# First attention stage in visits of two units: scores by head on half the rows of the array, no stacking by DMA

## The chip, the core and the metric

One core of one Trainium2 chip runs the whole program. The metric is the device time of the program in microseconds (us); for the kernel before, the median of three runs is 4077.31 us (4075.49 to 4078.02).

## What is computed

Sixteen samples of 512 tokens by 256 features pass through four blocks, each on a layer norm of its input and added to it. The change touches the first block alone:

```
x = x + attn_a(layernorm(x))      # 16 heads of width 64, gelu on the heads, then Wpost; X + P inside
x = x + ffn(layernorm(x))         # ternary weights, 256 -> 1024 -> 256
x = x + attn_b(layernorm(x))      # 16 heads of width 16, rotary, biases
x = x + ffn(layernorm(x))
...
Q, K, V = X @ Wq, X @ Wk, X @ Wv            # n, 512, 16, 64 each
attn = softmax(einsum('bshe,bthe->bsth', Q, K / 8), axis=2)
A = gelu(einsum('bsth,bthe->bshe', attn, V))
return X + A @ Wpost
```

## The kernel before

**Two stages.** The first stage does attn_a for all 16 samples and writes X1; the second does ffn, attn_b and ffn. Every engine runs one long loop over the same numbered slots, and each piece of work has a slot: `FIRST_A` to `LAST_A` for the first stage, from about slot 502 on also the opening of the second, whose scores begin at slot `SHIFT` = 554. Inside a slot the order is that of the code. Nothing reorders it, and engines wait for each other on semaphores.

**Units.** A sample has 8 pairs of heads; a pair has 4 units, a sample 32, the stage 512. Before, unit u of a pair is one head and one half of the queries (two blocks of 128). TensorE's slot s is: `a_scores(s + 3)` (4 matmuls of 512 columns), `a_transposes(s)` (8 of 128 columns, two banks), every fourth slot `a_values` of a whole pair (16 matmuls of 256 columns, which are 32 rows of the trace), then the products in `todo_of[s]`: queries or keys of a pair ("qk", 6 matmuls of 512), values of 128 tokens ("v", 6 of 512), transposed input ("x"), or the output product ("post", 24 of 256 columns for two blocks of tokens). Scores go to `ps_s`, four banks of PSUM, two to a unit, so that two units are in flight; everything else shares the three `banks`, filled in turn (`fill_of`), each waiting until the fill three before it is emptied.

**Exactness.** Products use fp32r parts: a high part and the rest. For the scores, ScalarE writes the high parts of q and k (L799) and VectorE the low parts (L972) to `raw_a`, with head 0 on partitions 0 to 63 and head 1 on 64 to 127. Six DMAs a pair (L364 to L366, `a_stack`) then build `stack_a`, where one head fills all 128 rows: high q above low q, against high k twice and low k twice. Two matmuls (L593, L594) give all four part products.

**The other engines, in slot s.** VectorE: `a_invert(s + 2)` (reciprocal of the sums, L954), the low parts or copies of the products of slot s - 1, `a_unit_max(s + 3)` (L947, 1024 columns), the copy of the first half of the transposed exponentials (L961, first of two banks), every fourth slot the copy of the values. ScalarE: the high parts or copies of slot s - 1, the copy of the second bank of transposed exponentials (L786), then `a_exps(s + 3)` (L775, two activations with running sums). GpSimd: the exponentials of unit s + 2 times the reciprocals (L495), which the transposes of slot s + 2 wait for. In this text the end of an instruction in a profile row is its start plus its duration.

## Time and profile before

| | |
|---|---|
| median of 3 runs | 4077.31 us |
| the profiled execution, its own time | 4078.41 us |
| its span, first to last instruction | 4076.6 us |
| mean granted TensorE clock | 0.981 of full |
| TensorE busy (matmuls overlap in this count) | 3760.2 us, 92% |
| first stage: last maximum taken (L947) | 2333.6 us |
| second stage: first maximum (L1088) | 2438.1 us |

The page slices the span in 40: TensorE is at 90% or more nearly everywhere but in the first slice and where the stages meet. Busy time counts a matmul from its start to the modelled end of its result, so neighbours overlap; how far one matmul is behind the last is read from the distance of their ends.

### The profile page before, as it was taken

Reading aid. Unit: us, or ns where it says so; the run is one execution under the profiler, and the core shown is the slowest. Engines: PE = TensorE matmul, PEld = TensorE weight load, DVE = VectorE, ACT = ScalarE, POOL = GpSimd, SP = SyncE. Lnnn points to the kernel's source line nnn. Section 1 sums busy time; section 2 is a strip of 40 time slices with the busy share of each in tenths; the row PEclk is TensorE's granted clock in tenths of the full one; section 3 lists DMA queues with packets and bytes.
Section 4 is the critical chain, followed back from the end, with each engine's and each line's share of the span. In section 5 each row is a group of like instructions: output and inputs, shape, how many; then the busy total and the mean of one; then the engine's idle time right before and its main releaser. Section 6 shows DMA issues by size and latency. Waiting matters only on the chain.

```text
span 4076.6 us, 64388 instructions
## 1 busy us (share of the span) xinstructions
PE 3760.2 (92%) x23170; PEld 2647.2 (65%) x23170; DVE 2718.1 (67%) x4275; ACT 2350.2 (58%) x4529; POOL 1930.6 (47%) x1219
## 2 busy tenths in 40 slices
PE   7999999999999999999999878999999999999987
PEld 5777777777777777777777654555555555555534
DVE  5665666666566666656666657777777777777762
ACT  4655655556555565555656535666666666666654
POOL 3454545445455455544544543444444444444412
PEclk9999999999999999999999978999999999999988
DMA  4443444434344344343443523232333332222220
GB/s 129 94 101 91 92 93 101 92 91 104 92 90 104 91 91 102 91 99 87 101 101 81 128 39 54 51 54 54 54 57 55 54 58 53 53 53 53 48 43 16
DMA packets 152363, 315.51 MB, mean 77 GB/s; under 512 B 23088, under 2 KB 76720, under 8 KB 152048
## 3 DMA queue, kind: packets, MB, share of 16 engines
q1 hardware_dynamic: 152048, 311.39, 35.6%
q8 instruction: 187, 3.06, 0.3%
q14 instruction: 128, 1.05, 0.1%
HBM read 33.43 MB, written 25.17 MB: 14 GB/s over the span
## 4 chain that ended last, share of the span: by engine, by line
PE 54%; DVE 21%; ACT 14%; issue 7%; POOL 3%; SPq 1%; DMA 0%; DVEq 0%; POOLq 0%; ACTq 0%
PE ps_o L622 10%; DVE neg_max L947 7%; ACT e_a L775 6%; PE ps_t L216 5%; PE ps_o L699 5%; DVE max_b L1088 4%; ACT raw_a L799 3%; PE ps_t L725 3%; PE ps_s L672 3%; PE ps_t L658 3%; PE ps_m L734 3%; PE ps_t L223 3%; PE ps_t L606 3%; PE ps_t L734 3%; POOL h_lo L529 2%
## 5 line engine op out<-in xcount | busy, mean ns | idle before, releaser
L495 POOL TENSOR_TENSOR e_a<-e_a,recip 128x1024 f32<-128x1024 f32 x512 | 970.4, 1895 | 1049.8 <-DVE recip L954 1049.8
L775 ACT ACTIVATE e_a<-ps_s,neg_max 128x512 f32<-128x512 f32 x1024 | 694.9, 684 | 245.0 <-DVE neg_max L947 234.1
L1088 DVE TENSOR_REDUCE max_b<-ps_s 128x2 f32<-128x1024 f32 x512 | 623.2, 1218 | 227.5 <-PE ps_s L672 225.1
L815 ACT ACTIVATE et<-ps_s 128x1024 f32<-128x1024 f32 x512 | 523.8, 1023 | 393.9 <-PE ps_s L686 393.8
L947 DVE TENSOR_REDUCE neg_max<-ps_s 128x2 f32<-128x1024 f32 x512 | 621.3, 1213 | 19.1 <-PE ps_s L594 19.1
L622 PE MATMUL ps_o<-et_a,v_a 128*64 128x256 f32 x4096 | 470.3, 382 | 0.0
L606 PE MATMUL ps_t<-ident,e_a 128*128 128x128 f32 x2736 | 394.7, 275 | 42.3 <-DVE et_a L961 36.1
L593 PE MATMUL ps_s<-stack_a 128*128 128x512 f32 x1024 | 412.7, 403 | 9.3 <-ACT e_a L775 7.7
L529 POOL TENSOR_TENSOR h_lo<-h,h_hi 128x512 fp32r<-128x512 f32 x256 | 327.2, 1296 | 168.8 <-ACT h_hi L859 168.8
L594 PE MATMUL ps_s<-stack_a 128*128 128x512 f32 x1024 | 401.9, 392 | 0.0
L606 PEld LDWEIGHTS ps_t<-ident,e_a 128*128 128x128 f32 x2736 | 321.2, 141 | 111.2 <-DVE et_a L961 52.1
L622 PEld LDWEIGHTS ps_o<-et_a,v_a 128*64 128x64 f32 x4096 | 282.5, 137 | 151.1 <-issue 21.4
L786 ACT ACTIVATE et_a<-ps_t 128x512 f32<-128x512 f32 x339 | 202.5, 597 | 297.1 <-PE ps_t L606 297.1
L954 DVE RECIPROCAL recip<-sums 128x2 f32<-128x2 f32 x512 | 84.7, 165 | 400.9 <-ACT e_a L775 400.9
L672 PE MATMUL ps_s<-k_stack,q_stack 48*128 48x512 f32 x1024 | 262.2, 508 | 91.8 <-DVE max_b L1088 91.5
L517 POOL TENSOR_TENSOR rstd<-rstd,minus_half 128x4 f32<-128x4 f32 x48 | 49.4, 1029 | 512.3 <-DVE rstd L1059 512.1
L699 PE MATMUL ps_o<-et,v_b 128*32 128x512 f32 x2048 | 283.6, 627 | 0.0
L972 DVE SCALAR_TENSOR_TENSOR raw_a<-ps_t,raw_a 128x512 fp32r<-128x512 f32 x171 | 118.3, 692 | 243.5 <-ACT raw_a L799 242.1
L672 PEld LDWEIGHTS ps_s<-k_stack,q_stack 48*128 48x128 f32 x1024 | 99.4, 188 | 257.6 <-issue 139.7
L961 DVE COPY et_a<-ps_t 128x512 f32<-128x512 f32 x345 | 235.0, 681 | 0.0
L593 PEld LDWEIGHTS ps_s<-stack_a 128*128 128x128 f32 x1024 | 192.8, 188 | 54.0 <-ACT e_a L775 13.1
L606 PE MATMUL ps_m<-ident,e_a 128*128 128x128 f32 x1360 | 207.3, 275 | 19.3 <-DVE et_a L961 16.9
(198 smaller groups left out, 7939.6 us busy)
## 6 DMA issues: line engine op xcount, KB each, us to landing
stack_a<-raw_a SPq DMA_DIRECT2D x256, 384.0 KB, 4.7
stack_a<-raw_a SPq DMA_DIRECT2D x256, 256.0 KB, 4.3
stack_a<-raw_a SPq DMA_DIRECT2D x256, 128.0 KB, 3.5
q_stack<-roped_q SPq DMA_DIRECT2D x256, 64.0 KB
k_stack<-roped_k SPq DMA_DIRECT2D x256, 64.0 KB
x_a<-X SPq DMA_DIRECT2D x16, 512.0 KB, 3.7
X<-x_a SPq DMA_DIRECT2D x16, 512.0 KB, 2.9
x_ahead<-X SPq DMA_DIRECT2D x16, 512.0 KB, 3.8
```

The lines of the kernel that those rows point to most:

```text
L495: nc.gpsimd.tensor_tensor(e_a[:, u % 4, :, :], e_a[:, u % 4, :, :], factor, ALU.mult).then_inc(e_normed, 1)
L529: nc.gpsimd.tensor_tensor(h_lo[:, i, :], h32[:, n % 4, :], h_hi[:, i, :], ALU.subtract).then_inc(h_split, 1)
L593: mm(out, st[:, 0, c:c + P], st[:, 1, :], start=True, stop=False)
L594: last = mm(out, st[:, 0, c:c + P], st[:, 2, :], start=False, stop=True)
L606: last = nc.tensor.transpose(bank(fill)[:, c:c + P], e_a[:, u % 4, j, t * P:(t + 1) * P], ident[:, :])
L622: last = mm(ps_o[HA * h:HA * (h + 1), half * HS:(half + 1) * HS], v_a[:, t, c:c + HA], et_a[:, (4 * n + 2 * half + h) % 5, t, :], start=(t ...
L672: last = mm(ps_s[:, score_bank(u) + h, :], q_stack[rows, pair, block_ * P:(block_ + 1) * P], k_stack[rows, pair, :], start=True, stop=True)
L699: last = mm(ps_o[32 * h:32 * (h + 1), :], v_b[:, s % 2, keys, 4 * quad + h, :], et[:, (2 * w + h // 2) % 5, h % 2, :], start=(keys == 0), ...
L775: ins = nc.scalar.activation(e_a[:, u % 4, j, :], ps_s[:, 2 * (u % 2) + j, :], ACT.Exp, bias=neg_max[:, u % 4, j:j + 1], accum_out=sums[:, ...
L815: nc.scalar.activation(et[:, v % 5, :, :], ps_s[:, 2:4, :], ACT.Exp)\
L947: nc.vector.reduce_max(neg_max[:, u % 4, :], ps_s[:, 2 * (u % 2):2 * (u % 2) + 2, :], AX.X, negate=True)\
L1088: nc.vector.reduce_max(max_b[:, u // 4 % 2, :, u % 4], ps_s[:, score_bank(u):score_bank(u) + 2, :], AX.X, negate=True).then_inc(max_done, 1)
```

## The change

**Visits.** A unit is now one block of 128 queries of both heads. `a_scores(u)` runs in even slots for units u and u + 1: per unit 6 matmuls with 64 rows each, head 0 on rows 0 to 63 and head 1 on rows 64 to 127, straight from `raw_a`, for three of the four part products (low times low is left out). `a_stack`, `stack_a` and their DMAs are gone. A visit writes all four banks of `ps_s`, so it waits until the exponentials of the unit before it are done (`a_exp_done >= u`), where before it waited for those of two units back. Values run in odd slots for two units (8 matmuls of 256 columns, 16 rows of a trace). `LEAD` = 4 takes the place of 3, and reciprocals and GpSimd's product stay at s + 2.

**Products.** Queries are made in slots 1 mod 4, keys in slots 2 mod 4, and values and output products in slots 0 and 3 mod 4, so that nearly every slot has one product of 6 or 12 matmuls; "post" is one block of tokens a fill. In slots 4 and 20 of a sample VectorE copies both banks.

**Setting up.** ScalarE casts four of the six pieces of the first weights. Input buffers are three. The weights of the ffn are loaded at slot 40, their sums taken at 471 and 473, their thresholds at 475 (509 before) and their quantising at 504 and 506 (509 and 510 before).

```diff
-        XT, QK_FIRST, VALUE_SLOTS = -10, -8, ((-6, -5, -2, -1), (3, 3, 7, 15))
-        POST = ((27, 31), (42, 43))
+        XT, QK_SLOTS = -9, (-7, -6)
+        FIRST_VALUES, VALUE_SLOTS = (-5, -4, -1, 0), ((-8, -5, -4, -1), (7, 8, 15, 16))
+        POST, LAST_POSTS = ((32, 32, 35, 36), (43, 44, 51, 52)), (45, 46, 47, 48)
...
+        GELUS, BOTH_TURNED = (19, 35), (4, 20)
...
-        LOAD_W1, LOAD_W2, LOAD_WB, SPLIT, ABS = 500, 503, 506, (511, 512), (503, 506)
-        GAMMA, QUANTISE, SCALE, CLEAR = 508, (509, 510), 514, (513, 514)
-        FIRST_SPLIT, SPLIT_OF_PAIR = (-12, -9, -6, -5, -4, -3), ((1, 2), (4, 5))
+        LOAD_W, LOAD_WB, LOAD_REST, SPLIT, ABS = 40, 484, 503, (508, 509), (471, 473)
+        GAMMA, QUANTISE, SCALE, CLEAR = 474, (504, 506), 514, (513, 514)
+        FIRST_CAST, FIRST_SPLIT, SPLIT_OF_PAIR = (None, None, -8, -5, -4, 5), (-11, -8, -7, -4, -2, 6), ((1, 2), (4, 5))
...
                 def a_scores(u):
-                    n, half, h = u // 4, u // 2 % 2, u % 2
+
+                    n = u // 4
                     if u % 4 == 0:
-                        pe.wait_ge(stacked[n % 2], (n // 2 + 1) * 6 * 16)
-                    if u >= 2:
-                        pe.wait_ge(a_exp_done, u - 1)
-                    st = stack_a[:, n % 2, h, :, :]
+                        for i in range(2):
+                            wait_emptied(pe, fill_of["qk", n % PAIRS, i, n // PAIRS])
+                    if u:
+                        pe.wait_ge(a_exp_done, u)
+                    raw = raw_a[:, n % 2, :, :]
                     for j in range(2):
-                        c = (2 * half + j) * P
-                        out = ps_s[:, 2 * (u % 2) + j, :]
-                        mm(out, st[:, 0, c:c + P], st[:, 1, :], start=True, stop=False)
-                        last = mm(out, st[:, 0, c:c + P], st[:, 2, :], start=False, stop=True)
-                    last.then_inc(a_qk_done, 1)
+                        c = (u % 4 + j) * P
+                        for m, (q_part, k_part) in enumerate(((0, 2), (0, 3), (1, 2))):
+                            for h in range(2):
+                                rows = slice(HA * h, HA * (h + 1))
+                                last = mm(ps_s[:, 2 * j + h, :], raw[rows, q_part, c:c + P], raw[rows, k_part, :],
+                                          start=(m == 0), stop=(m == 2))
+                        last.then_inc(a_qk_done, 1)
...
-                        if 0 <= slot + 3 < UNITS_ALL:
-                            a_scores(slot + 3)
+                        if slot % 2 == 0 and 0 <= slot + LEAD < UNITS_ALL:
+                            a_scores(slot + LEAD)
+                        if slot % 2 == 1 and 3 <= slot < UNITS_ALL:
+                            a_values((slot - 3) // 2)
+                        if slot == UNITS_ALL:
+                            a_values(UNITS_ALL // 2 - 1)
                         if 0 <= slot < UNITS_ALL:
                             a_transposes(slot)
-                        if slot % 4 == 0 and 1 <= slot // 4 <= PAIRS * BATCH:
-                            a_values(slot // 4 - 1)
...
-                        if 0 <= slot < UNITS_ALL:
+                        if 0 <= slot < UNITS_ALL and slot % UNITS not in BOTH_TURNED:
                             a_copy_turned(slot)
-                        if 0 <= slot + 3 < UNITS_ALL:
-                            a_exps(slot + 3)
+                        if 0 <= slot + LEAD < UNITS_ALL:
+                            a_exps(slot + LEAD)
...
-                        if 0 <= slot + 2 < UNITS_ALL:
-                            a_invert(slot + 2)
+                        if slot % 2 == 1 and 0 <= slot + LEAD < UNITS_ALL:
+                            a_unit_max(slot + LEAD)
+                        if 0 <= slot + LEAD - 2 < UNITS_ALL:
+                            a_invert(slot + LEAD - 2)
                         for todo in todo_of.get(slot - 1, []):
                             a_low(todo)
-                        if 0 <= slot + 3 < UNITS_ALL:
-                            a_unit_max(slot + 3)
+                        if slot % 2 == 0 and 0 <= slot + LEAD < UNITS_ALL:
+                            a_unit_max(slot + LEAD)
```

TensorE in the middle of the stage, before: a slot with scores of one unit, transposes and the values of a whole pair, and the product after them (`stack_a` holds the stacked parts, `et_a` the transposed exponentials).

```order
L593 MATMUL ps_s<-stack_a 128x512
L594 MATMUL ps_s<-stack_a 128x512
L593 MATMUL ps_s<-stack_a 128x512
L594 MATMUL ps_s<-stack_a 128x512
L606 MATMUL ps_t<-ident,e_a 128x128 x8
L622 MATMUL ps_o<-et_a,v_a 64x256 x16
L216 MATMUL ps_m<-xh_a,wa_hi 128x512
L216 MATMUL ps_m<-xh_a,wa_lo 128x512
L216 MATMUL ps_m<-xh_a,wa_hi 128x512
L216 MATMUL ps_m<-xh_a,wa_lo 128x512
L216 MATMUL ps_m<-xl_a,wa_hi 128x512 x2
L593 MATMUL ps_s<-stack_a 128x512
```

TensorE there in the changed kernel: an even slot (scores of two units, transposes, keys), then an odd slot up to its product.

```order
L592 MATMUL ps_s<-raw_a 128x512 x12
L605 MATMUL ps_t<-ident,e_a 128x128 x8
L216 MATMUL ps_m<-xh_a,wa_hi 128x512
L216 MATMUL ps_m<-xh_a,wa_lo 128x512
L216 MATMUL ps_m<-xh_a,wa_hi 128x512
L216 MATMUL ps_m<-xh_a,wa_lo 128x512
L216 MATMUL ps_m<-xl_a,wa_hi 128x512 x2
L623 MATMUL ps_o<-et_a,v_a 64x256 x8
L605 MATMUL ps_t<-ident,e_a 128x128 x8
L223 MATMUL ps_m<-wa_hi,xh_a 128x512
```

Scores of two units now stand together every second slot, with values of two units in the slots between, and one product stands between the odd slot's transposes and the next scores.

ScalarE at the same place, before:

```order
L775 ACTIVATE e_a,sums<-ps_s,neg_max 128x512 x2
L799 ACTIVATE raw_a<-ps_t 128x512
L786 ACTIVATE et_a<-ps_m 128x512
L775 ACTIVATE e_a,sums<-ps_s,neg_max 128x512 x2
L786 ACTIVATE et_a<-ps_m 128x512
```

ScalarE in the changed kernel:

```order
L777 ACTIVATE e_a,sums<-ps_s,neg_max 128x512 x2
L803 ACTIVATE raw_a<-ps_m 128x512
L784 ACTIVATE et_a<-ps_t 128x512
L777 ACTIVATE e_a,sums<-ps_s,neg_max 128x512 x2
L803 ACTIVATE raw_a<-ps_m 128x512
```

The kinds stand in the same order: the copy of the transposed exponentials (L786, now L784) goes ahead of the exponentials of its slot in both. What moved is what waits for them: the exponentials of an odd slot now release the next scores.

VectorE, before, three slots:

```order
L954 RECIPROCAL recip<-sums 128x2
L972 SCALAR_TENSOR_TENSOR raw_a<-ps_t,raw_a 128x512
L947 TENSOR_REDUCE neg_max<-ps_s 128x2
L961 COPY et_a<-ps_t 128x512
L954 RECIPROCAL recip<-sums 128x2
L947 TENSOR_REDUCE neg_max<-ps_s 128x2
L961 COPY et_a<-ps_t 128x512
```

VectorE in the changed kernel, an even slot from its low part on, and the odd slot after it:

```order
L981 SCALAR_TENSOR_TENSOR raw_a<-ps_t,raw_a 128x512
L956 TENSOR_REDUCE neg_max<-ps_s 128x2
L970 COPY et_a<-ps_t 128x512
L999 COPY heads_a<-ps_o 128x512
L956 TENSOR_REDUCE neg_max<-ps_s 128x2
L963 RECIPROCAL recip<-sums 128x2
L981 SCALAR_TENSOR_TENSOR raw_a<-ps_t,raw_a 128x512
L970 COPY et_a<-ps_t 128x512
```

In odd slots the maximum (L956) has moved ahead of the reciprocal and of the low part.

## Rows read from the trace of the kernel before

**Rows 1.** The page: busy us (share of the span) and instructions; one costly group.

```profile
PE 3760.2 (92%) x23170; PEld 2647.2 (65%) x23170; DVE 2718.1 (67%) x4275; ACT 2350.2 (58%) x4529; POOL 1930.6 (47%) x1219
...
L947 DVE TENSOR_REDUCE neg_max<-ps_s 128x2 f32<-128x1024 f32 x512 | 621.3, 1213 | 19.1 <-PE ps_s L594 19.1
```

**Rows 2.** Busy time by stretch, second sample: PE, PEld, DVE, ACT, POOL, clock, DMA.

```profile
182.20:327.20 145.00, 137.48 (x889) 107.50 (x888) 90.92 (x153) 84.39 (x193) 74.33 (x42) 1.00 0.42 95
```

**Rows 3.** TensorE's waits, 100 to 2230 us: us in total, times, longest.

```profile
PE ps_t L606 <- DVE et_a L961: 31.7, 60, 0.7
...
PE ps_s L593 <- DMA stack_a<-raw_a: 0.2, 1, 0.2
```

**Rows 4.** Timeline of TensorE: the same matmul eleven samples apart (start, duration).

```profile
557.02 0.50 PE L593 MATMUL ps_s<-stack_a 128*128 128x512 f32 x1 [0.23 <-ACT e_a L775]
...
2151.87 0.50 PE L593 MATMUL ps_s<-stack_a 128*128 128x512 f32 x1 [0.23 <-ACT e_a L775]
```

**Rows 5.** Timeline of TensorE: product, scores of a unit, transposes.

```profile
1003.78 0.62 PE L216 MATMUL ps_t<-xl_a,wa_hi 128*128 128x512 f32 x2
...
1004.93 0.40 PE L594 MATMUL ps_s<-stack_a 128*128 128x512 f32 x1
...
1005.60 0.60 PE L606 MATMUL ps_m<-ident,e_a 128*128 128x128 f32 x4
```

**Rows 6.** Timeline of TensorE: into the values of a pair and out.

```profile
1012.72 0.66 PE L606 MATMUL ps_m<-ident,e_a 128*128 128x128 f32 x4 [0.31 <-DVE et_a L961]
1013.31 3.67 PE L622 MATMUL ps_o<-et_a,v_a 128*64 128x256 f32 x32
1016.92 0.50 PE L216 MATMUL ps_t<-xh_a,wa_hi 128*128 128x512 f32 x1
```

**Rows 7.** Timeline of TensorE, second stage: matmuls of 48 and 50 rows in twos.

```profile
3002.50 0.27 PE L742 MATMUL ps_t<-ident,max_b 128*8 128x128 f32 x1
3002.70 0.50 PE L672 MATMUL ps_s<-k_stack,q_stack 48*128 48x512 f32 x2
3003.04 0.40 PE L686 MATMUL ps_s<-q_stack,k_stack 50*128 50x512 f32 x2
```

**Rows 8.** Timeline of TensorE, second stage: values in column quarters, then transposes.

```profile
2595.78 1.06 PE L699 MATMUL ps_o<-et,v_b 128*32 128x512 f32 x8
2596.77 0.66 PE L719 MATMUL ps_t<-ident,xn 128*128 128x128 f32 x4
```

**Rows 9.** Timeline of TensorE: transposes, and the last of 24 output matmuls.

```profile
1026.65 0.60 PE L606 MATMUL ps_m<-ident,e_a 128*128 128x128 f32 x4
...
1029.84 0.28 PE L658 MATMUL ps_t<-wpost_hi,heads_parts 128*128 128x256 f32 x1
```

**Rows 10.** Timeline of ScalarE just after: the copy, then a unit's exponentials.

```profile
1027.29 0.60 ACT L786 ACTIVATE et_a<-ps_m 128x512 f32<-128x512 f32 x1 [0.43 <-PE ps_m L606]
1027.78 0.68 ACT L775 ACTIVATE e_a<-ps_s,neg_max 128x512 f32<-128x512 f32 x1
...
1029.02 0.21 ACT L775 ACTIVATION_READ_ACCUMULATOR e_a<-ps_s,neg_max 128x1 f32 x1
```

**Rows 11.** Timeline: the end of a unit's exponentials, ahead of 557.02 above.

```profile
556.77 0.20 ACT L775 ACTIVATION_READ_ACCUMULATOR e_a<-ps_s,neg_max 128x1 f32 x1
```

**Rows 12.** Timeline at the start: VectorE's low part, then TensorE.

```profile
18.69 0.69 DVE L972 SCALAR_TENSOR_TENSOR raw_a<-ps_t,raw_a 128x512 fp32r<-128x512 f32 x1 [1.64 <-ACT raw_a L799]
```

**Rows 13.** Timeline of TensorE at the start: first value product, first transposes.

```profile
22.99 0.77 PE L223 MATMUL ps_t<-wa_hi,xh_a 128*128 128x512 f32 x1 [4.96 <-DVE wa_lo L927]
```

**Rows 14.** The same, slot 0.

```profile
41.17 0.73 PE L606 MATMUL ps_t<-ident,e_a 128*128 128x128 f32 x4
```

**Rows 15.** Timeline of TensorE: transposes of slots 480 and 504.

```profile
2212.08 0.60 PE L606 MATMUL ps_m<-ident,e_a 128*128 128x128 f32 x4
...
2315.08 0.60 PE L606 MATMUL ps_m<-ident,e_a 128*128 128x128 f32 x4
```

**Rows 16.** Timeline of TensorE where the stages meet: slot 511, first "up" product.

```profile
2345.98 1.11 PE L606 MATMUL ps_t<-ident,e_a 128*128 128x128 f32 x4 [5.38 <-DVE xl L1131]
...
2358.05 0.74 PE L725 MATMUL ps_m<-xh,w 128*128 128x512 f32 x2
```

**Rows 17.** Timeline of VectorE there: one quantising pass.

```profile
2342.37 2.35 DVE L1028 SCALAR_TENSOR_TENSOR w<-w_raw,half_gamma,w 128x2048 fp32r<-128x2048 f32 x1
```

223 lines of the change are left out of this document (111 added, 112 removed).

## The prediction, made before the changed kernel ran

> **What bounds the kernel now.** I read the busy times first: TensorE has 92% [rows 1], and in one sample of the first stage 137.5 of 145.0 us [rows 2]. That count overlaps, so the next view is the timeline, where I take distances between the ends of matmuls. The same matmul stands at 557.02 and at 2151.87 us, eleven samples apart [rows 4]: 1594.85 / 11 = 144.99 us a sample. The stage repeats to a few hundredths, so it can be summed.
>
> Pitches: 512 columns take 0.23 us (1004.40 to 1004.63, and scores of a unit end at 5.33: 4 in 0.93) [rows 5]. Eight transposes take 6.20 - 5.33 = 0.87, 0.109 each. Twenty-four output matmuls take 1030.12 - 1027.25 = 2.87, 0.12 each [rows 9]. The values of a pair take 1016.98 - 1013.38 = 3.60 [rows 6]. Their 32 rows are 16 steps; with a step of 0.216 the first costs 0.36, so 0.14 goes for entering the mode with two column halves, and the product behind ends its first matmul 0.44 later where 0.23 is usual: 0.21 for leaving it.
>
> A sample's work on TensorE before, then: 32 x (0.93 + 0.87) + 8 x 3.81 = 88.1 for scores, transposes and values; 24 products of 6 x 0.23 = 1.38 (16 queries and keys, 8 values) = 33.1; output 96 x 0.12 = 11.5; x 8 x 0.11 = 0.9. Sum 133.6. The other 11.4 us are waits, and the table of waits shows the main one: transposes that wait until VectorE has emptied a bank [rows 3], in slots with little work on TensorE. The stacking DMAs cost almost nothing (0.2 us) [rows 3].
>
> **The change part by part.**
>
> *Scores.* Two units took 1.86 us. Now there are six steps of two matmuls on half the rows each. That such twos run side by side the second stage shows: two matmuls end at 3003.20 and the next two at 3003.44, a step of 0.24 [rows 7]. Entering costs: the first two end 0.43 after a 128-column matmul, 0.19 more than a step. Leaving a tiled mode for transposes: the four end at 2597.43, 0.59 after the values; less 3 x 0.109 the first took 0.26, so 0.15 more [rows 8]. Sum: 0.43 + 5 x 0.24 + 0.15 = 1.78. Gain 0.08 for two units, of the quarter of the matmuls that the change drops.
>
> *Values.* 0.36 + 7 x 0.216 + 0.15 = 2.02 for two units, where half of 3.81 is 1.90: loss 0.12, since the mode is entered twice as often. Together TensorE's work is 0.04 us a pair of slots larger, 16 x 0.04 = 0.6 a sample: 134.2. Products are only moved. So any gain has to come from the 11.4 us of waits.
>
> The Trainium skill, TensorEngine Tiling (Array Packing), Key Properties, gives row tiling up to twice the speed, but says that changing the mode drains TensorE. The trace agrees that both hold (0.24 for two, 0.15 to 0.21 at a change).
>
> *Old waits.* They go: with scores and values in turn and one product of 1.38 to 1.44 us in nearly every slot, no slot is as short as the bare 1.80 us of scores and transposes, and VectorE's copy (after a 1.21 us maximum [rows 1]) comes before the bank is needed.
>
> *The new wait.* Scores of slot s + 2 need all four banks of `ps_s`, so the exponentials of the odd slot s + 1 must be done. ScalarE does them behind the copy of that slot's second bank, which needs the last transpose of slot s + 1. On TensorE only the odd product (1.38) stands between. This ring is closed by waits alone, whatever slack the engines have:
> - last transpose to start of copy: 1027.25 to 1027.29, 0.04 [rows 9, 10];
> - copy to exponentials behind it: 0.49 [rows 10];
> - exponentials to the end of their sum: 1027.78 to 1029.23, 1.45 [rows 10];
> - that end (556.97) to the end of the first score matmul (557.52): 0.55 [rows 4, 11].
>
> In all 2.53. Without the wait it would be 1.38 + 0.43 = 1.81, so 0.72 us stand idle in each pair of slots, 16 x 0.72 = 11.5 a sample, as much as the old waits were. The whole ring: 2.53 + 5 x 0.24 (less 0.01 of rounding in the step, 1.19) + transposes 0.26 + 7 x 0.109 = 1.02, + the even product, + values 1.87 + transposes 1.02 = 7.63 + even product. Even products of a sample: 8 keys and 4 values of 1.38, 5 output blocks of 1.44: 23.7. A sample: 16 x 7.63 + 23.7 = 145.8, against 145.0. From slot 32 to slot 480 are 14 samples: **+11 us**.
>
> *The opening.* Slot 0 transposes at 41.17 [rows 14]. Value weights were split by VectorE alone, and TensorE waited 4.96 us until 22.99 [rows 13]. ScalarE's casts take that wait away, and the scores no longer wait for DMAs: the low part of the first keys is there at 19.38 [rows 12], the first scores go behind one value product at about 20.6. Two rounds of score, maximum, second maximum behind a split, exponentials (1.0 + 1.2 + 1.2 + 2 x 1.45 + 0.5, about 7 each) and one visit of 1.6 lead to 36: **-5 us** (bounds -2 and -8). Slots 0 to 32 then lack five output blocks on the ring and have one value product more: 16 x 7.63 + 17.9 = 140.0, where 182.2 - 41.2 = 141.0 were [rows 2, 14]: **-1**.
>
> *The end.* From slot 480 [rows 15] the ring takes 12 x 7.63 + 18.2 = 109.8 to slot 504, where 2315.08 - 2212.08 = 103.0 were: +7. From 504 to the first "up" 43.0 passed [rows 15, 16], with TensorE waiting 5.38 at once behind thresholds and quantising (2.35 for one of its passes [rows 17]). Now these lie under slots 475 to 506, where a quantising of 3.6 delays the second maximum by some 1.6 in each of two visits: 2 x 9.2 + some 12 for slots 508 to 511 = 30, **-13**. Together **-6** (bounds +1 and -12). Behind that nothing changes: the second stage keeps its order, and the same 48 output matmuls come there.
>
> Third input buffer, earlier loads of X and of weights, smaller output adds, two more bank copies on VectorE: nothing, since VectorE is busy 91 of 145 us and ScalarE 84 [rows 2]. If that cover fails it shows in the ring, below.
>
> **Sum.** +11 - 5 - 1 - 6 = -1 on 4078.4, the profiled execution's own time; the median of the runs is 1.1 below that. I predict **4076 us**: no change that a measurement of this kernel can tell, which needs about 0.2% or 8 us.
>
> **The rivals.**
>
> *Faster by a shorter ring.* The ring turns 256 times, so 0.05 us in it is 13 us. Its softest term is the step of two matmuls: 0.24 [rows 7], but tiled values step at 0.216 for the same streaming time [rows 6]. With that: 5 x 0.024 x 256 = 31 less, 4045. For it: tiled mode. Against: the one row of the same kind. The ends of the two openings, both guessed short of work, add up to 9 more. Chance 0.24.
>
> *The change does what its layout suggests.* If the exponentials do not gate the next visit, a sample falls to 134.2: 15 x 10.8 + 7 = 170 less, 3906. It needs the odd product to cover 2.1 us (2.53 - 0.43); it is 1.44 at most. Chance 0.03.
>
> *Slower: the heads of visits.* A visit of values now waits for four bank copies and, every second time, for the copy of the last values; the changes of mode are eight in four slots where there were two. If leaving and entering a mode on the ring (three times in a pair of slots) costs the 0.21 seen behind the values [rows 6] and not 0.14 to 0.15, this adds 3 x 0.06 x 256 = 46: 4122; half of it, 4099. It decides from 0.03 us a turn on. Against: rows 8 show the very change into transposes. The Trainium skill, TensorE: Matmul & The Clock Gate, Single matmul latency, gives a fixed cost of 166 ns at full clock for a matmul that nothing overlaps; taken as the price of a change, an estimate from that page is 3 x 0.02 x 256 = 15 us more. Chance 0.23.
>
> *Slower: VectorE late for the values.* The values wait until the last ones are copied out of `ps_o`. I find that copy done some 0.4 us before TensorE comes, once in four slots. With VectorE 1 us later it costs 0.6 x 128 = 77: 4153. Chance 0.08.
>
> **How the numbers follow.** The forecast has 0.42, within 8 us. Faster has 0.24 + 0.03 and slower 0.23 + 0.08, about 0.27 and 0.31. The range leaves out the 170 and the 77 and some of each end: 4045 to 4110.
>
> **What the profile after would show.** A sample of 145.8 us from one score matmul to the same 32 units on; every even slot's first score matmul waiting about 0.6 us for ScalarE's exponentials; nearly no wait of transposes for VectorE's copy; twos of score matmuls 0.24 apart; slot 0 at 36 and first "up" near 2357. I am wrong if the ring is not closed as I wrote it (scores released by something else), or if a sample is off by over 0.6 us.

## The result, and the profile after

| | before | after |
|---|---|---|
| median, timed side by side | 4076.40 us (4 runs, 4075.45 to 4078.02) | 4102.61 us (4 runs, 4100.78 to 4107.73) |
| span of the profiled execution | 4076.6 us | 4099.0 us |
| granted TensorE clock | 0.981 | 0.981 |

The ratio is 1.0066, with a 95% interval of 1.0048 to 1.0083: the kernel is slower by 26 us, where 4076 and no measurable change were forecast. The time lies inside the range of 4045 to 4110. The two profiled executions are 22.4 us apart; the other 4 us between the medians lie in runs without a profile.

The page after: busy times, the chain that ended last, and the group that answers to L947 of [rows 1].

```profile
PE 3725.7 (91%) x24194; PEld 2520.5 (61%) x24194; DVE 2733.9 (67%) x4367; ACT 2299.7 (56%) x4501; POOL 1921.2 (47%) x1219
...
PE 68%; ACT 12%; DVE 12%; issue 5%; POOL 3%; DMA 0%; ACTq 0%; DVEq 0%; POOLq 0%
...
L956 DVE TENSOR_REDUCE neg_max<-ps_s 128x2 f32<-128x1024 f32 x512 | 623.3, 1217 | 159.7 <-PE ps_s L592 159.7
```

VectorE sat idle 19.1 us ahead of its maxima before [rows 1] and sits idle 159.7 now, for scores. ScalarE has 12% of the chain that ended last. The second sample by stretch, as in [rows 2], and TensorE's waits from 100 to 2230 us (total, times, longest), as in [rows 3]:

```profile
174.70:321.10 146.40, 135.31 (x955) 99.55 (x953) 91.88 (x159) 80.77 (x191) 73.88 (x43) 1.00 0.03 8
```

```profile
PE ps_s L592 <- ACT e_a L777: 157.0, 225, 2.1
PE ps_s L592 <- DVE v_a L988: 5.0, 7, 0.7
```

A sample takes 146.4 us (145.0 before), the DMA share fell from 0.42 to 0.03, and the transposes no longer wait for VectorE. One wait is left: the score matmuls (L592) for ScalarE's exponentials (L777), at the head of nearly every visit. It is the ring that the prediction describes: a chain of waits that comes back to its own start once in every two slots. Here it is closed twice, in TensorE's timeline and ScalarE's (start, duration), from an odd slot's transposes to the next scores:

```profile
1205.69 0.60 PE L605 MATMUL ps_m<-ident,e_a 128*128 128x128 f32 x4
...
1208.32 1.66 PE L592 MATMUL ps_s<-raw_a 64*128 64x512 f32 x12 [0.63 <-ACT e_a L777]
1209.91 0.65 PE L605 MATMUL ps_t<-ident,e_a 128*128 128x128 f32 x4
...
1214.69 0.60 PE L605 MATMUL ps_m<-ident,e_a 128*128 128x128 f32 x4
...
1217.41 0.74 PE L592 MATMUL ps_s<-raw_a 64*128 64x512 f32 x4 [0.69 <-ACT e_a L777]
```

```profile
1206.33 0.60 ACT L784 ACTIVATE et_a<-ps_m 128x512 f32<-128x512 f32 x1 [3.83 <-PE ps_m L605]
1206.83 0.68 ACT L777 ACTIVATE e_a<-ps_s,neg_max 128x512 f32<-128x512 f32 x1
...
1208.06 0.21 ACT L777 ACTIVATION_READ_ACCUMULATOR e_a<-ps_s,neg_max 128x1 f32 x1
...
1217.06 0.21 ACT L777 ACTIVATION_READ_ACCUMULATOR e_a<-ps_s,neg_max 128x1 f32 x1
```

The transposes end at 1206.29, the copy starts at 1206.33, the exponentials at 1206.83, their sum ends at 1208.27, the scores start at 1208.32. The next visit differs in one thing: sum at 1217.27, scores at 1217.41, 0.14 behind it and not 0.05. Over the stage's 255 visits behind the first the two kinds take turns, but for one visit: 126 with 0.143 to 0.145, 128 with 0.052 or 0.053. The first kind is the one in which `a_scores` also waits for the emptied query and key banks.

**Where the 22.4 us between the spans are**, from the first transposes of slots 0, 32, 480 and 504, the first "up" and the first maximum of the second stage:

| stretch | before | after | difference | forecast |
|---|---|---|---|---|
| start to slot 0 | 41.2 | 33.9 | -7.3 | -5 |
| slot 0 to 32 | 141.1 | 140.8 | -0.3 | -1 |
| 32 to 480, 14 samples | 2029.8 | 2049.6 | +19.8 | +11 |
| 480 to 504 | 103.0 | 110.7 | +7.7 | +7 |
| 504 to the first "up" | 43.0 | 43.3 | +0.3 | -13 |
| to the second stage's first maximum | 80.1 | 82.1 | +2.0 | 0 |
| rest | 1638.5 | 1638.6 | +0.1 | 0 |

Two forecasts failed: the samples by 9 us, and the end by 15. The opening is less certain than its line looks. From slot 0 to slot 32 the kernels of experiments 5 to 8 run the same code as this one; two of them took 140.7 us at a granted clock of 1.00, as here, and two 143.3 and 143.4 at 0.98.

The end, VectorE and GpSimd after, where [rows 16] and [rows 17] stood before:

```profile
2350.42 2.35 DVE L1037 SCALAR_TENSOR_TENSOR w<-w_raw,half_gamma,w 128x2048 fp32r<-128x2048 f32 x1
...
2357.01 2.35 DVE L1011 CAST wb_hi<-wb_raw 128x768 fp32r<-128x768 f32 x2
...
2359.94 5.29 DVE L1016 TENSOR_TENSOR wb_lo<-wb_raw,wb_hi 128x768 fp32r<-128x768 f32 x2
```

```profile
2359.51 1.89 POOL L486 TENSOR_TENSOR e_a<-e_a,recip 128x1024 f32<-128x1024 f32 x1 [1.04 <-DVE recip L963]
2361.36 3.05 POOL L516 TENSOR_TENSOR x_ahead<-x_ahead,b_rows 128x1024 f32<-128x1024 f32 x1
```

Quantising no longer stands at the very end, but the split does (5.29 us for two subtractions), and TensorE's transposes of slot 510 wait 5.9 us behind it:

```profile
PE ps_s L592 <- ACT e_a L777: 7.0, 4, 3.6
PE ps_t L605 <- DVE xl L1140: 5.9, 1, 5.9
PE ps_t L605 <- DVE et_a L970: 2.5, 1, 2.5
```

These are TensorE's waits from 2310 to 2385 us. Its clock differs there too. Busy time by stretch, before and after, with the granted clock as the third number from the end:

```profile
2315.00:2358.00 43.00, 32.38 (x236) 24.88 (x233) 34.90 (x51) 14.12 (x34) 18.10 (x12) 0.92 0.35 96
2335.00:2378.00 43.00, 29.25 (x187) 20.84 (x187) 29.39 (x39) 11.33 (x26) 15.44 (x9) 0.82 0.03 6
```

With levels of 1.2 and 2.4 GHz, 0.82 means that TensorE ran some 15 us of these 43 at the lower one, and 0.92 some 7; after, each of these stretches begins in or just behind a wait of 2.1 to 5.9 us. Two groups of matmuls on the chain that ended last show the price: scores of 2.61 us, and values of 3.48 us behind the wait of 5.9, where 1.66 and 1.95 are usual.

```profile
2343.57 2.61 PE L592 MATMUL ps_s<-raw_a 64*128 64x512 f32 x12 [3.60 <-ACT e_a L777]
...
2368.13 3.48 PE L623 MATMUL ps_o<-et_a,v_a 128*64 128x256 f32 x16
```

### The profile page after: what moved, and what is told of

It is laid out like the page before. It is cut to its first block, busy times and chain, and to the rows that moved or that the text cites. A ratio compares the mean times of both kernels' runs of the same rounds, so it can differ in the third digit from the quotient of the medians.

```text
span 4099.0 us, 65128 instructions
## 1 busy us (share of the span) xinstructions
PE 3725.7 (91%) x24194; PEld 2520.5 (61%) x24194; DVE 2733.9 (67%) x4367; ACT 2299.7 (56%) x4501; POOL 1921.2 (47%) x1219
## 4 chain that ended last, share of the span: by engine, by line
PE 68%; ACT 12%; DVE 12%; issue 5%; POOL 3%; DMA 0%; ACTq 0%; DVEq 0%; POOLq 0%
PE ps_o L623 12%; PE ps_s L592 10%; ACT e_a L777 9%; PE ps_t L605 8%; PE ps_o L699 4%; DVE max_b L1097 4%; PE ps_m L605 4%; PE ps_t L216 4%; PE ps_t L734 4%; PE ps_s L672 3%; PE ps_t L725 2%; PE ps_t L658 2%; PE ps_m L216 2%; PE ps_s L686 2%; PE ps_m L725 2%
## 5 line engine op out<-in xcount | busy, mean ns | idle before, releaser
L956 DVE TENSOR_REDUCE neg_max<-ps_s 128x2 f32<-128x1024 f32 x512 | 623.3, 1217 | 159.7 <-PE ps_s L592 159.7
L777 ACT ACTIVATE e_a<-ps_s,neg_max 128x512 f32<-128x512 f32 x1024 | 692.1, 686 | 9.9 <-DVE neg_max L956 9.5
L592 PE MATMUL ps_s<-raw_a 64*128 64x512 f32 x3072 | 427.1, 408 | 184.5 <-ACT e_a L777 179.3
L784 ACT ACTIVATE et_a<-ps_t 128x512 f32<-128x512 f32 x299 | 179.0, 599 | 652.4 <-PE ps_t L605 652.4
L623 PE MATMUL ps_o<-et_a,v_a 128*64 128x256 f32 x4096 | 501.1, 387 | 2.4 <-DVE heads_a L999 1.7
L592 PEld LDWEIGHTS ps_s<-raw_a 64*128 64x128 f32 x3072 | 291.6, 185 | 305.9 <-ACT e_a L777 140.6
L623 PEld LDWEIGHTS ps_o<-et_a,v_a 128*64 128x64 f32 x4096 | 274.1, 137 | 191.0 <-issue 73.1
L970 DVE COPY et_a<-ps_t 128x512 f32<-128x512 f32 x366 | 252.1, 691 | 203.6 <-PE ps_t L605 199.3
L605 PEld LDWEIGHTS ps_t<-ident,e_a 128*128 128x128 f32 x2660 | 291.3, 141 | 139.0 <-issue 121.9
L784 ACT ACTIVATE et_a<-ps_m 128x512 f32<-128x512 f32 x181 | 108.4, 599 | 398.9 <-PE ps_m L605 398.9
L734 PE MATMUL ps_t<-w,h_hi 128*128 128x256 f32 x752 | 203.1, 305 | 25.9 <-POOL h_lo L522 25.7
L605 PE MATMUL ps_m<-ident,e_a 128*128 128x128 f32 x1436 | 224.8, 279 | 0.0
```

Of the source, the lines that this page charges most:

```text
L592: last = mm(ps_s[:, 2 * j + h, :], raw[rows, q_part, c:c + P], raw[rows, k_part, :], start=(m == 0), stop=(m == 2))
L605: last = nc.tensor.transpose(bank(fill)[:, c:c + P], e_a[:, u % 5, j, t * P:(t + 1) * P], ident[:, :])
L623: last = mm(out, v_a[:, t, c:c + HA], et_a[:, 2 * (q % 2):2 * (q % 2) + 2, t, h, :], start=(t == 0), stop=(t == TB - 1))
L734: last = mm(half, hidden[:, f, tokens], w2[:, f, :], start=(f == 0 and m == 0), stop=(f == FT - 1 and m == 1))
L777: ins = nc.scalar.activation(e_a[:, u % 5, h, :], ps_s[:, 2 * (u % 2) + h, :], ACT.Exp, bias=neg_max[:, u % 5, h:h + 1], accum_out=sums[:, ...
L956: nc.vector.reduce_max(neg_max[:, u % 5, :], ps_s[:, 2 * (u % 2):2 * (u % 2) + 2, :], AX.X, negate=True)\
```

## The experiments

All but one start from the kernel after. Each was timed beside the kernel before, whose medians were 4078.6 to 4080.2 us here and 4076.4 in the result above. Times of different series can so be compared to about 4 us, and the ratio to the kernel before stands beside each. The sample that is given is the mean from slot 32 on, without the stage's last.

**1. Exponentials first.** Two lines of ScalarE's loop change places, in odd slots.

```diff
+                        if slot % 2 == 1 and 0 <= slot + LEAD < UNITS_ALL:
+                            a_exps(slot + LEAD)
                         if 0 <= slot < UNITS_ALL and slot % UNITS not in BOTH_TURNED:
                             a_copy_turned(slot)
-                        if 0 <= slot + LEAD < UNITS_ALL:
+                        if slot % 2 == 0 and 0 <= slot + LEAD < UNITS_ALL:
                             a_exps(slot + LEAD)
```

> The kernel after, but in odd slots ScalarE does the exponentials ahead of its copy of turned exponentials (in even slots the copy stays first). Theory (the sample's length is set by a ring: last transpose, ScalarE's copy, exponentials, end of their sum, first score matmul, then TensorE's work up to the next last transpose): the last transposes and the copy leave the ring, TensorE stops waiting 1.1 us each second slot, a sample falls from 146.4 to 134 to 137 us, and the time to 3930 to 3970 us. Rival A (the second maximum, not the copy, holds the exponentials): a sample stays at 145 to 147, the time at 4090 to 4105. Rival B (the copy is now late by the 1.1 to 1.4 us of the exponentials, and the values or the next transposes wait for it on TensorE, since the bank that it frees is wanted back): the wait only changes its name to ScalarE's copy, a sample of 141 to 150, the time 4030 to 4150.

Measured: 3929.1 us, ratio 0.9632 (0.9618 to 0.9647). The second sample and the largest of TensorE's waits from 100 to 2230 us:

```profile
161.30:296.50 135.20, 134.62 (x955) 98.66 (x953) 91.95 (x159) 81.99 (x191) 73.98 (x43) 1.00 0.03 9
```

```profile
PE ps_s L592 <- ACT e_a L777: 8.8, 3, 6.2
PE ps_m L658 <- POOL heads_parts L490: 5.2, 1, 5.2
```

The theory holds. A sample takes 135.1 us, and the wait of 157.0 us is gone but for the end. What was moved is only the order of two instructions on an engine that is 56% busy; the mean durations of the costly groups changed by 1% or less (an exponential takes 692 ns, 686 before). One small group did not: VectorE's cast for the output product takes 602 ns and not 508. ScalarE's rows show the new order: the exponentials of the odd slot start 2.0 us ahead of the copy, before that slot's last transposes are done.

```profile
1212.59 0.70 ACT L777 ACTIVATE e_a<-ps_s,neg_max 128x512 f32<-128x512 f32 x1
...
1213.25 0.71 ACT L777 ACTIVATE e_a<-ps_s,neg_max 128x512 f32<-128x512 f32 x1
...
1214.58 0.60 ACT L784 ACTIVATE et_a<-ps_t 128x512 f32<-128x512 f32 x1 [0.53 <-PE ps_t L605]
```

**2. The second wait of the visit's head, a slot earlier.**

```diff
 def a_scores(u):
-    if u % 4 == 0:
+    if u == 0:
         for i in range(2):
-            wait_emptied(pe, fill_of["qk", n % PAIRS, i, n // PAIRS])
+            wait_emptied(pe, fill_of["qk", 0, i, 0])
...
 a_transposes(slot)
+if slot % 4 == 3 and 0 < slot + 5 < UNITS_ALL:
+    n = (slot + 5) // 4
+    for i in range(2):
+        wait_emptied(pe, fill_of["qk", n % PAIRS, i, n // PAIRS])
```

> The kernel after, but the wait for the two emptied query and key banks, which stood at the head of every other visit together with the wait for the exponentials, is made on TensorE one slot earlier, behind the transposes of the odd slot before. Theory (the second wait at the head costs 0.064 us in each visit that has it, on the ring): 128 x 0.064 = 8 us less, 4094 us; first score matmul of those visits 0.054 behind the sum's end and not 0.144. Rival (the 0.064 comes from what TensorE did before, products of half width, and not from the second wait): no change, 4102, the first score matmul still 0.11 to 0.15 behind the sum's end. Second rival: the banks are emptied late, and the earlier wait holds the products of that slot: slower, 4110 or more.

Measured: 4096.8 us, ratio 1.0047 (1.0034 to 1.0059). In time that is 6 us less, near the edge of what five runs tell. The trace is sharper: 248 of 255 visits now start 0.053 us behind the sum, and a sample takes 145.58 us, 0.81 less (8 x 0.09 = 0.72 by the two distances). The 14 samples are 11.2 us shorter; slot 32 comes 5.9 us later, half of it between slots 0 and 32 at a granted clock of 0.98 and not 1.00, which hides part of the gain. So the wait at the head costs 0.09 us of its own, although the banks had long been empty. With it gone the ring is 0.2 us a sample from what was forecast (145.8).

**3. and 4. A shorter product beside the ring, and one in it.** For the queries (b = 0, third experiment) or the keys (b = 1, fourth), two matmuls of six (the low parts are left out, so the products are less exact):

```diff
-last = feature_major(bank(fill), xh_a, xl_a, wa_hi, wa_lo, b * DA + a * P)
+if b == 0:
+    for k in range(KT):
+        last = mm(bank(fill), wa_hi[:, k, b * DA + a * P:b * DA + a * P + P], xh_a[:, k, :],
+                  start=(k == 0), stop=(k == KT - 1))
+else:
+    last = feature_major(bank(fill), xh_a, xl_a, wa_hi, wa_lo, b * DA + a * P)
```

> The kernel after, but of the queries' product, which stands in an odd slot behind the last transposes, 2 matmuls of 6 are done (those of the high parts alone; the low parts of queries' input and weights are left out). Theory (ring): that product lies beside the ring, behind the last transpose and ahead of the wait for the exponentials, and not in it; TensorE only waits 0.9 us more there: a sample of 146 to 147 as before, the time 4095 to 4103. Rival (TensorE's own work sets the sample): 4 x 0.23 = 0.92 us less in 8 visits a sample, 139 a sample, 4103 - 118 = 3985 us.

Measured: 4104.9 us, ratio 1.0065 (1.0047 to 1.0084), a sample of 146.4, and the wait for exponentials grew from 157.0 to 254.6 us. 118 us of TensorE's work taken away give nothing: that work lies beside the ring, and TensorE's busy time as such does not bound the stage.

> The kernel after, but of the keys' product, which stands in an even slot between the score matmuls and the transposes of the odd slot, 2 matmuls of 6 are done (those of the high parts alone; the low parts are left out). Theory (ring): that product is in the ring, so all of it counts: 4 x 0.23 = 0.92 us less in 8 visits a sample, 146.4 - 7.4 = 139.0 a sample, the time 4103 - 118 = 3985 us. Rival (VectorE's maxima or copies set the sample, and TensorE's work is hidden): less than half of it, 4045 us or more.

Measured: 4076.4 us, ratio 0.9997 (0.9987 to 1.0007), a sample of 144.58. Only 1.8 of the 7.4 us a sample came back, less than half, as the rival had it. TensorE's waits, and VectorE's and TensorE's rows at one odd slot:

```profile
PE ps_s L592 <- ACT e_a L782: 139.3, 204, 2.1
PE ps_o L623 <- DVE heads_a L1004: 49.9, 88, 0.6
PE ps_o L623 <- ACT et_a L789: 25.6, 30, 1.0
PE ps_s L592 <- DVE v_a L993: 21.7, 30, 0.7
```

```profile
1212.81 1.21 DVE L961 TENSOR_REDUCE neg_max<-ps_s 128x2 f32<-128x1024 f32 x1
1214.01 0.69 DVE L975 COPY et_a<-ps_t 128x512 f32<-128x512 f32 x1
1214.62 0.68 DVE L1004 COPY heads_a<-ps_o 128x512 f32<-128x512 f32 x1
```

```profile
1214.16 0.71 PE L647 MATMUL ps_t<-xh_a,wa_hi 128*128 128x512 f32 x2
1215.44 0.87 PE L623 MATMUL ps_o<-et_a,v_a 128*64 128x256 f32 x6 [0.57 <-DVE heads_a L1004]
```

The keys' product covered VectorE's copies between the scores and the values of the next slot. With 0.92 us of cover gone the values wait 0.57 for the copy out of `ps_o`: a second limit stands some 0.35 us behind the ring in these slots (0.92 - 0.57, an estimate). This is the prediction's last rival, VectorE late for the values, which found that copy some 0.4 us early.

**5. to 8. The end.** First, the last sample's output products put in among its last visits, and the split of the second stage's weights three slots earlier:

```diff
-where = LAST_POSTS if late(s, half) else POST[half]
+where = LAST_POSTS if late(s, half) else (27, 29, 30, 31) if (s, half) == (BATCH - 1, 0) else POST[half]
```

> The kernel after, but the output products of the last sample's first half stand in the slots 27, 29, 30 and 31 of that sample (507, 509, 510 and 511) and not in 512, 512, 515 and 516. Theory (24 of these 48 matmuls lay behind the last unit ahead of the first ups, 24 among the ups, and the last visits' waits hide them where they are put now): 48 x 0.12 = 5.7 us less, 4097 us, the first up 3 us nearer to the last unit. Rival (the end waits for VectorE's low part of the last inputs, not for TensorE's work, so that only the place of the wait changes): within 2 us of 4102.6.

Measured: 4110.9 us, ratio 1.0078 (1.0066 to 1.0091), on the wrong side of both. TensorE's waits at the end:

```profile
PE ps_s L592 <- ACT e_a L777: 4.9, 1, 4.9
PE ps_t L605 <- DVE x_a L993: 4.5, 1, 4.5
PE ps_m L605 <- DVE xl L1140: 2.0, 1, 2.0
PE ps_t L658 <- DVE xl L1140: 1.9, 1, 1.9
```

An output product fills a bank that VectorE must add out (L993), and that add stands behind the 5.29 us of the split. By the trace the second stage begins 3.2 us later for it. Another 7 us of this run lie in the second stage, whose code is the same; they are told of below.

```diff
-        LOAD_W, LOAD_WB, LOAD_REST, SPLIT, ABS = 40, 484, 503, (508, 509), (471, 473)
+        LOAD_W, LOAD_WB, LOAD_REST, SPLIT, ABS = 40, 484, 503, (505, 507), (471, 473)
```

> The kernel after, but VectorE splits the second stage's weights in slots 505 and 507, not in 508 and 509. Theory (in the kernel after, the cast took 2.35 us and the subtraction 5.29, beside GpSimd's instructions, against 1.02 and 1.82 in the kernel before; the transposes of slot 510 waited 5.9 us for VectorE behind it): with the two kinds farther apart the cast takes 1.0 to 1.3 and the subtraction 1.8 to 3, the wait at slot 510 falls below 2 us, and the time to 4096 to 4099. Rival A (VectorE is full from 504 on: quantising, 3.7 us a piece, fills it anyway): the maxima of slots 505 to 508 come later by what the splits take, and the time stays within 2 us of 4102.6 or goes up by as much as 5. Rival B (the long duration belongs to the instruction and its operands' places, not to GpSimd): still 2.35 and 5.29.

Measured: 4098.5 us, ratio 1.0049 (1.0036 to 1.0062). The rows of VectorE:

```profile
2344.69 1.88 DVE L1011 CAST wb_hi<-wb_raw 128x768 fp32r<-128x768 f32 x1
...
2358.75 1.81 DVE L1016 TENSOR_TENSOR wb_lo<-wb_raw,wb_hi 128x768 fp32r<-128x768 f32 x2
```

The subtractions take 0.94 us each where no GpSimd instruction runs beside them, and rival B falls. The cast met one even here (1.88 us for the first of two that take 1.02 together alone). The wait at slot 510 fell from 5.9 to 2.0 us, and from the transposes of slot 504 to the first "up" 39.0 us pass, not 43.3.

Then the quantising too, moved behind the last maximum:

```diff
-        LOAD_W, LOAD_WB, LOAD_REST, SPLIT, ABS = 40, 484, 503, (508, 509), (471, 473)
-        GAMMA, QUANTISE, SCALE, CLEAR = 474, (504, 506), 514, (513, 514)
+        LOAD_W, LOAD_WB, LOAD_REST, SPLIT, ABS = 40, 484, 503, (504, 506), (471, 473)
+        GAMMA, QUANTISE, SCALE, CLEAR = 474, (509, 510), 514, (513, 514)
```

> The kernel after with VectorE's jobs of the last slots in another order: the weights are split in slots 504 and 506 (2.3 us together where GpSimd is idle, up to 7.6 beside it), and the feed-forward weights quantised in 509 and 510, behind the last maximum (slot 507), and not in 504 and 506. Theory (quantising, 3.6 us a piece, delays the maxima of slots 504 to 507, so that TensorE waits 3.6 and 2.1 us for exponentials; behind the last maximum it only holds copies and the low part of the last inputs, as it did in the kernel before): those two waits fall to 1.2 and less, the first up 3 to 6 us earlier against the rest of the stage, 4095 to 4100. Rival (the work is the same, and what it no longer holds at 504 it holds at 509 and 510): within 2 us of 4102.6, waits of 3 us or more for VectorE's copies at slots 509 to 511.

Measured: 4099.9 us, ratio 1.0050 (1.0037 to 1.0064); the stretch takes 41.8 us. The waits for exponentials fell as the theory says (5.5 us in all, none above 2.1), but VectorE's jobs now meet GpSimd's (a second quantising pass takes 4.31 us beside it, 2.35 alone) and hold the last inputs' low part for longer. It is the rival that came out, in this row:

```profile
PE ps_t L605 <- DVE xl L1140: 6.8, 1, 6.8
```

Last, the work itself: the second pass of each quantising is left out, so the feed-forward weights are no longer the reference's.

```diff
-link(nc.vector.tensor_scalar(out, flat, half_gamma[:, 1, i:i + 1], None, ALU.is_lt))
-nc.vector.scalar_tensor_tensor(out, flat, half_gamma[:, 0, i:i + 1], out, ALU.is_gt, ALU.subtract)\
-    .then_inc(weights_ready, 1)
+nc.vector.tensor_scalar(out, flat, half_gamma[:, 1, i:i + 1], None, ALU.is_lt).then_inc(weights_ready, 1)
```

> The kernel after, where quantising does only its first pass of two for each weight matrix (the second, 2.35 us on VectorE each in slots 504 and 506, is left out, so the weights of the feed-forward layers aren't the reference's). Theory (VectorE sets the end of the first stage from slot 504 on): of 4.7 us at least 3 come back between the transposes of slot 504 and the first up (43.3 in the kernel after), 4096 to 4100, and TensorE's waits of 3.6 and 2.1 us for the exponentials there fall to 1.3 and less. Rival (TensorE's own work, half of it at a granted clock of 0.8, sets it and the waits are made up for elsewhere): 43.3 within 1 us, the time within 2 us of 4102.6.

Measured: 4094.2 us, ratio 1.0041 (1.0027 to 1.0055). The stretch takes 38.5 us: of 4.7 us taken from VectorE, 4.8 came back, at the same granted clock (0.82). So VectorE's work counts in full there. The waits for exponentials fell from 5.7 to 2.5 us, not to 1.3; the wait for the low part stayed at 5.9 us, since the split was not touched. The amount of work is not all of it: VectorE is busy 26.0 us in this stretch in experiment 6 and 26.1 in experiment 7, and they take 39.0 and 41.8 us. Its jobs' places count too.

**9. and 10. Two parts of the change undone**, each on the kernel after.

```diff
-a_normalise_exps(slot + LEAD - 2)
+a_normalise_exps(slot + LEAD - 1)
...
-a_invert(slot + LEAD - 2)
+a_invert(slot + LEAD - 1)
```

> The kernel after with one part of the change undone: the reciprocals (VectorE) and the multiplications by them (GpSimd) one slot earlier. Theory (the ring doesn't run through the reciprocals: they are done two slots ahead of the transposes, and VectorE finds the sums ready within 0.2 us of the end of its maximum): a sample of 146.0 to 146.8, the time 4098 to 4108. Rival (VectorE now stops for the exponentials with its copies and maxima queued behind it, which was the reason for the later slot): waits of VectorE for ScalarE of 0.5 us or more a slot, a sample of 148 or more, 4130 us or more.

Measured: 4106.0 us, ratio 1.0062 (1.0047 to 1.0077), a sample of 146.37. VectorE does stop for the exponentials, 389.2 us in all, and the sample shows that TensorE is not held by it.

```diff
-if slot % 2 == 1 and 0 <= slot + LEAD < UNITS_ALL:
-    a_unit_max(slot + LEAD)
...
-if slot % 2 == 0 and 0 <= slot + LEAD < UNITS_ALL:
+if 0 <= slot + LEAD < UNITS_ALL:
     a_unit_max(slot + LEAD)
```

> The kernel after with one part of the change undone: the second maximum of a visit isn't first in its slot on VectorE, but behind the reciprocal and the low parts, as the first one is. Theory (the exponentials of odd slots start at the end of ScalarE's copy, 2.8 us behind the end of their maximum, so 0.15 to 0.85 us on it are hidden): a sample of 146.2 to 146.8, the time 4100 to 4106. Rival (the maximum is the gate that the profile doesn't name): up to 128 x 0.7 = 90 us more, 4130 us or more.

Measured: 4108.7 us, ratio 1.0068 (1.0051 to 1.0084), a sample of 146.28. The time is above the 4100 to 4106 of the theory, but this isn't in the samples. The profiled execution is 11 us longer: 6 us up to slot 32, half of it from slot 0 on at a granted clock of 0.98, then 2 less up to the second stage, and 7 in that stage, whose code is the same. Neither part does anything to a sample while the ring is closed.

**11. The kernel before, exponentials first in every slot.**

```diff
+if 0 <= slot + 3 < UNITS_ALL:
+    a_exps(slot + 3)
 if 0 <= slot < UNITS_ALL:
     a_copy_turned(slot)
-if 0 <= slot + 3 < UNITS_ALL:
-    a_exps(slot + 3)
```

> The kernel before, with ScalarE's exponentials ahead of its copy of turned exponentials in every slot, as the one edit. Theory (in the kernel before no ring ran through the exponentials; TensorE waited for VectorE's copies and for its own order, 11.4 us a sample, and a later copy on ScalarE can only hold the values): no gain, a sample of 145 to 150, the time 4070 to 4150. Rival (the order copy first costs either kernel the same): the sample falls to 135 to 138, the time to 3930 to 3970 as in the kernel after.

Measured: 4228.0 us, ratio 1.0365 (1.0346 to 1.0384), a sample of 154.3. ScalarE's largest wait there, and the same wait in the kernel before:

```profile
ACT e_a L775 <- DVE neg_max L947: 743.8, 413, 4.5
```

```profile
ACT e_a L775 <- DVE neg_max L947: 201.9, 251, 1.4
```

The edit that takes 4% from the kernel after adds 4% to the kernel before. There every slot makes the scores, the maximum and the exponentials of one unit in turn, so exponentials in front wait for the maximum of their own slot, and the copy with its bank waits behind them. ScalarE's rows show the first; how it reaches TensorE is argued, since TensorE's listed waits from 100 to 2230 us grew by only some 60 us (113 to 173), of which 29 are for that copy. In the kernel after, an odd slot's scores are made a slot earlier. It is worse than the 4150 of the theory, whose direction was right. Which part of the change (two units a visit, `LEAD` of 4, the earlier second maximum) makes the order bearable was argued here, not told apart.

**12. Exponentials first in even slots too.**

```diff
+if 0 <= slot + LEAD < UNITS_ALL:
+    a_exps(slot + LEAD)
 if 0 <= slot < UNITS_ALL and slot % UNITS not in BOTH_TURNED:
     a_copy_turned(slot)
-if 0 <= slot + LEAD < UNITS_ALL:
-    a_exps(slot + LEAD)
```

> The kernel after, with ScalarE's exponentials ahead of its copy in every slot, even slots too. Theory (in an even slot the exponentials wait for the first maximum, 2.9 us behind the first score matmul, so the copy behind them ends about 4.9 us behind it, where the transposes of the odd slot want its bank at 4 to 6): slower than with odd slots alone, TensorE waits for ScalarE's copy, 3950 to 4060 us. Rival (it has slack enough): 3925 to 3935, as with odd slots alone. Other rival (the copy of even slots joins a ring of its own): above 4102.

Measured: 3925.5 us, ratio 0.9620 (0.9601 to 0.9639), a sample of 135.14, the same as with odd slots alone. The rival with slack enough came out. By the order of the code, the bank of the even slot's copy is not wanted back before the odd slot's transposes are through, with values and a product between.

**13. to 15. Together.** Experiments 1, 2 and 5:

> Three edits on the kernel after together: exponentials ahead of the copy in odd slots, the wait for the query and key banks made a slot earlier, and the last sample's first output products in slots 507 to 511. Theory (with the ring open TensorE hardly waits, 35 us in the whole first stage, so the second edit has nothing left to shorten, and the third takes 3 to 6 us at the end): 3923 to 3928, against 3929 for the first edit alone. Rival (the ring was only loosened, and its second wait still counts): 3915 to 3920. Other side: the early wait holds TensorE where it has no slack now, 3932 or more.

Measured: 3933.8 us, ratio 0.9643 (0.9628 to 0.9657). The other side came out, but for experiment 5's reason: the waits for the add of the output product (3.9 us) and for the low part (3.9) are in this trace too, and a sample is unchanged (135.17). Experiments 1 and 6:

> The two edits that gained alone, together on the kernel after: exponentials ahead of the copy in odd slots, and the second stage's weights split in slots 505 and 507. Theory (the one works in all sixteen samples, the other in the last eight slots, and they share no wait): 3929 - 4 = 3925, within 3921 to 3929, and the subtraction of the split at 0.94 us apiece. Rival (with the ring open TensorE reaches the end sooner than VectorE, which is then the one that is late there, so that the split's place counts otherwise): 3931 or more.

Measured: **3920.4 us**, ratio 0.9609 (0.9595 to 0.9624), 4% below the kernel before and the fastest here, 0.6 us under the range of the theory. From slot 504 to the first "up" 41.1 us pass, 45.7 in experiment 1, and the subtractions take 0.94 us each. Then the quantising last and the split in 504 and 506:

> The fastest so far (exponentials ahead of the copy in odd slots, split in slots 505 and 507; 3920) with quantising moved behind the last maximum (509 and 510) and the split to 504 and 506. Theory: the one wait of 6.2 us for the exponentials at slot 504 falls to 1 or 2, 3914 to 3918. Rival (the copies of slots 509 to 511 now wait for VectorE): 3918 to 3924.

Measured: 3925.3 us, ratio 0.9624 (0.9611 to 0.9637). Against the one before, the intervals overlap and the first "up" stands at 2197.7 and at 2197.0: no gain, as experiment 7 lets one expect. The time is outside both the theory's 3914 to 3918 and the rival's 3918 to 3924. The wait for exponentials fell from 6.2 only to 3.5 us, and the one for the low part rose from 2.0 to 7.2.

## Why the prediction was wrong, step by step

- *What bounds the kernel, pitches, TensorE's work.* Right. In the rows above, the scores end at 1209.98, four transposes 0.58 later, where 0.26 + 3 x 0.109 = 0.59 was worked out. TensorE's work was put at 134.2 us a sample; with the ring open a sample takes 135.1, which leaves costly changes of mode 0.9 us of the 2.9 that this rival gave them, at most.
- *Old waits, new wait.* Right: the first went, the second came, with the four pieces 0.04, 0.50, 1.44 and the start behind the sum.
- *The ring's length.* This term was mis-sized, since the end of the sum to the first score matmul was read at one visit of the kernel before and taken for all. In every second visit the head has a second wait, which costs 0.09 us. Experiment 2 takes it out and finds 145.58, where 145.8 was forecast. In the kernel after it is 146.39, just inside the 0.6 us that the prediction allowed itself: +19.8 us for 14 samples, not +11.
- *The rival with the shorter ring (0.24), and the one in which the exponentials don't gate (0.03).* The first did not come. The second is excluded for this kernel by the 157.0 us, but its price was near: a sample of 134.2 and a time of 3906 were worked out, and experiment 1 measured 135.1 and 3929. The prediction saw that the copy stands ahead of the exponentials and summed it as fixed. It didn't ask which of the two has slack, which the trace before couldn't show but the ring's own list could: the copy is wanted a slot later than the exponentials.
- *The opening.* -7.3 where -5 with bounds of -2 and -8 was given. Right. That slots 0 to 32 came out within 1 us is in part luck: the same code took 2.6 us more in two other executions, at a lower granted clock.
- *480 to 504.* +7.7 where +7 was given. Right.
- *504 to the first "up".* This is the step that failed: -13 was forecast and +0.3 came. It summed TensorE's visits (2 x 9.2 + 12) and let VectorE's jobs vanish beneath the maxima. The split of the weights, moved from 511 and 512 to 508 and 509, isn't in the sum at all; it took 7.6 us, where it took 2.8 before. Experiment 6, which takes most of that back, shortens the stretch by 4.3 us, and experiment 8 shows what VectorE's work costs there: 4.7 us less work, 4.8 us less time. VectorE is busy 29.4 of the 43 us, and what it does comes in chains with TensorE (scores, maximum, exponentials), so that the other jobs lengthen the chains. The sum also took TensorE at full clock. The lower clock costs 2.5 us in the two groups shown above, a part of the miss that no experiment took out by itself.
- *The same 48 output matmuls.* 24 of them come ahead of the first "up" (2375.29 to 2378.26 us), and the sum for the end leaves out these 3.0 us. Experiment 5 shows that putting them among the last visits costs, since each needs VectorE. With the 4.3 us of the split and the 2.5 of the clock this makes some 10 of the 13 us, an estimate, since the three may overlap; the rest stays open.
- *The sum.* +11 - 5 - 1 - 6 = -1 was forecast, +19.8 - 7.3 - 0.3 + 10.0 = +22.2 came, and 0.1 behind it. The forecast's own chance for slower, 0.31, stood on other mechanisms than the two that decided.

## What to carry to other kernels

When the profile shows one wait repeated at the head of each round, write down the ring that closes it and ask of every instruction in it whether the next round needs it, or whether it only stands in front; here one exchange of two instructions on a half-idle engine was worth 4%. An order that is best in one schedule can be the worst in another, so try it again after the stage is rebuilt. Where stages meet, sum every engine, not just the busiest: the engine that does the odd jobs there can be the bound, and the granted clock there need not be the one of the steady stage.

## What the runs showed of the hardware

**VectorE and GpSimd on SBUF.** VectorE's subtraction of two SBUF tensors, 128x768, took 0.94 us with GpSimd idle. Beside GpSimd it took 2.28 and 3.09. The first started at 2359.94; GpSimd's multiplication ended at 2361.40, and 0.94 later is 2362.34, where the first ended at 2362.22. GpSimd's addition, 2.35 us alone (experiment 6), took 3.05. These durations fit, within 0.2 us, an engine that waits for the other's whole instruction and then takes its usual time. The Trainium skill, SBUF — State Buffer, section SBUF: two separate sides, describes a port pair of the two engines that one of them holds for its whole instruction; the trace agrees, with these numbers.

**A wait that is long met still costs.** The second wait at the head of a visit took 0.09 us on TensorE, on semaphores that had been raised. VectorE's row for the last of these banks ends at 1214.18, and the scores start at 1217.41:

```profile
1213.49 0.69 DVE L981 SCALAR_TENSOR_TENSOR raw_a<-ps_t,raw_a 128x512 fp32r<-128x512 f32 x1 [0.40 <-ACT raw_a L803]
```

Without it the same visits lose the 0.09 us (experiment 2).

**The second stage's samples come in two lengths.** Its code is the same in every kernel here, yet from its first maximum on it took 1638.6 us in the kernel after and 1645.5 in experiment 5. Two of its samples after, busy time by stretch with the granted clock as the third number from the end:

```profile
2635.91:2735.56 99.65, 93.95 (x561) 55.62 (x562) 77.02 (x114) 62.20 (x91) 46.65 (x34) 1.00 0.30 54
2735.56:2836.73 101.17, 95.46 (x561) 56.65 (x562) 77.03 (x114) 62.20 (x91) 46.66 (x34) 0.98 0.30 53
```

Where the clock granted is 0.98, a sample takes 1.5 us more: some stretch of it ran at 1.2 GHz and not at 2.4. After has 3 such samples, experiments 5 and 10 have 5, and their last full window is longer (92.5 us against 90.05). What brings the lower clock on in a given sample no run shows. Differences of 5 us between kernels that touch only the first stage can come from this alone, so for those the trace's own stretches say more than the time.
